# A graph layer on one TensorE: rounds of edges set around the halves of layer 1 and layer 2, with a reordered front and a last block of one part

## The reference, cut to what matters

```python
agg = segment_sum(edge_attr, receivers, num_segments=6250)      # 106250 edges x 128, receivers sorted
h   = relu(layernorm(x))                                        # 6250 nodes x 128
out = x + relu(concatenate([agg, h], axis=1) @ W1 + b1) @ W2 + b2   # W1 256x512, W2 512x128
```

## Time and profile before

| | before |
|---|---|
| median of 3 runs | 207.87 us (207.56 to 207.99) |
| the profiled execution, its own time | 207.57 us |
| its span, first to last instruction | 205.8 us |
| PE busy | 193.6 us, 94% |
| DVE busy | 131.8 us, 64% |
| ACT busy | 85.6 us, 42% |
| POOL busy | 44.5 us, 22% |
| DMA moved | 62.49 MB, mean 304 GB/s |
| granted TensorE clock, mean | 0.993 of full |

### The profile page before, as it was taken

One profiled execution on the slowest core, in us unless ns is written; L12 is line 12 of the kernel. 1 busy time (PEld: TensorE's weight loads), 2 busy tenths in 40 slices (PEclk: granted clock), 3 DMA queues, 4 the chain that ended last, 5 costly groups with the idle time before them and its releaser, 6 DMA issues.

```text
span 205.8 us, 6846 instructions
## 1 busy us (share of the span) xinstructions
PE 193.6 (94%) x2580; PEld 166.7 (81%) x2580; DVE 131.8 (64%) x582; ACT 85.6 (42%) x187; POOL 44.5 (22%) x121
## 2 busy tenths in 40 slices
PE   5979699999999999999999999999998999999990
PEld 5668588887898898898887987988987988978990
DVE  2665948776778669577677777786782884853200
ACT  3324434643714713823634544337137137126030
POOL 6973022102210220222022022012202012200000
PEclk9999999999999999999999999999999999999997
DMA  6999999999999999999999999999998970010100
GB/s 210 380 375 376 361 374 377 377 374 384 385 377 385 377 372 392 377 379 389 376 392 377 381 386 377 371 347 372 348 376 311 299 250 12 3 52 0 51 24 21
DMA packets 44497, 62.49 MB, mean 304 GB/s; under 512 B 1796, under 2 KB 44168, under 8 KB 44462
## 3 DMA queue, kind: packets, MB, share of 16 engines
q1 hardware_dynamic: 44132, 61.66, 84.5%
q10 hardware_dynamic: 330, 0.36, 0.7%
HBM read 58.81 MB, written 3.20 MB: 301 GB/s over the span
## 4 chain that ended last, share of the span: by engine, by line
PE 82%; DMA 7%; POOL 3%; DVE 2%; ACT 2%; issue 1%; DVEq 0%; POOLq 0%
PE bank L916 22%; PE bank L850 20%; PE bank L887 17%; PE bank L897 16%; DMA edges<-in_edge_attr 6%; PE bank L861 4%; PE bank L871 2%; DMA hidden<-in_dst 2%; POOL aggT L390 1%; POOL rstd L370 1%; PE bank L843 1%; ACT hidden L448 1%; DVE aggT L617 1%; POOL var L365 1%; ACT xn L417 0%
## 5 line engine op out<-in xcount | busy, mean ns | idle before, releaser
L850 PE MATMUL bank<-edges,onehot 128*32 128x128 f32 x1656 | 52.5, 277 | 1.4 <-DMA edges<-in_edge_attr 0.9
L850 PEld LDWEIGHTS bank<-edges,onehot 128*32 128x32 f32 x1656 | 43.6, 110 | 8.2 <-issue 5.0
L617 DVE TENSOR_TENSOR aggT<-bank,aggT 128x32 f32 x277 | 35.7, 190 | 22.3 <-issue 10.3
L448 ACT ACTIVATE hidden<-bank,b_col 128x512 f32<-128x512 f32 (+2 forms) x56 | 34.2, 633 | 36.8 <-PE bank L897 36.7
L916 PE MATMUL bank<-w,hidden 128*128 128x128 f32 (+1 forms) x400 | 48.4, 278 | 0.0
L916 PEld LDWEIGHTS bank<-w,hidden 128*128 128x128 f32 (+1 forms) x400 | 45.8, 189 | 2.5 <-issue 2.2
L417 ACT ACTIVATE xn<-xs,shift,rstd 128x128 f32<-128x128 f32 (+1 forms) x50 | 21.8, 484 | 49.2 <-POOL shift L372 49.2
L365 POOL TENSOR_SCALAR var<-meanvar 128x2 f32<-128x2 f32 (+1 forms) x25 | 8.4, 334 | 128.2 <-DVE meanvar L544 128.1
L524 DVE TENSOR_TENSOR onehot<-relT,iota 128x384 f32<-128x384 f32 x69 | 34.5, 550 | 0.0
L897 PE MATMUL bank<-agg_hi,w_hi 128*128 128x512 f32 (+2 forms) x56 | 21.6, 385 | 1.6 <-DVE agg_lo L566 1.6
L887 PE MATMUL bank<-hT_hi,w_hi 128*128 128x512 f32 (+2 forms) x56 | 22.1, 394 | 0.2 <-DVE hT_lo L560 0.2
(11 more groups left out here) (101 smaller groups left out, 181.3 us busy)
## 6 DMA issues: line engine op xcount, KB each, us to landing
edges<-in_edge_attr SPq DMA_DIRECT2D x69, 768.0 KB, 10.6
xs<-in_x SPq DMA_DIRECT2D x21, 128.0 KB, 9.7
out_rows<-w SPq DMA_DIRECT2D x5, 256.0 KB, 10.1
out_rows<-outrow SPq DMA_DIRECT2D x5, 256.0 KB, 9.9
w<-in_L_gnn_W SPq DMA_DIRECT2D x3, 256.0 KB, 10.6
out_rows<-outrow SPq DMA_DIRECT2D x3, 128.0 KB, 8.4
xs<-in_x SPq DMA_DIRECT2D x1, 256.0 KB, 5.8
hidden<-in_dst SPq DMA_DIRECT2D x1, 192.0 KB, 3.1
```

What stands on the lines that cost most here:

```text
L448: nc.scalar.activation(hidden[:, t, 0:cols], hidden_of(s, t), ACT.Relu, bias=b1_col[:, t:t + 1]).then_inc(hidden_ready, 1)
L617: nc.vector.tensor_tensor(win, turn_ps[:, at:at + W], win, ALU.add).then_inc(agg_added, 1)
L850: ins = nc.tensor.matmul(sums_ps[t * W:(t + 1) * W, cols], onehot[:, hots, e, :], edges[:, slot, e * F:(e + 1) * F], start=(g == 0), stop= ...
```

## The change

Three things. In steps 5 to 24 one round comes first, then half of layer 2 or of `layer1_h`, then the other rounds, then the second half. The front (steps 0 to 4, with ACT's, DVE's and POOL's order there) is reordered: six idle transposes go, layer 2 of groups 1 and 2 is cut in two parts around a step's end, and POOL clears less before the second block's statistics. The last block gets one node to a partition: one part of 106 rows, and its store is 96 rows and 10 rows. The wait for `over_read` moves behind the first round of step 20.

```diff
-    assert NLAST % 2 == 0 and NB % 2 == 1
+    assert NLAST <= P and NB % 2 == 1
+    LAST_CUT = NLAST // 16 * 16
     def width(b):
-        return NLAST // 2 if isinstance(b, int) and b == NB - 1 else P
+        return NLAST if isinstance(b, int) and b == NB - 1 else P
+    def parts(b):
+        return 1 if isinstance(b, int) and b == NB - 1 else 2
...
-                    sp.dma_start(out_last_v, rows[0:width(NB - 1), 1, :]).then_inc(done, 16)
+                    sp.dma_start(out_last_v[0:LAST_CUT, :], rows[0:LAST_CUT, 1, 0:F]).then_inc(done, 16)
+                    sp.dma_start(out_last_v[LAST_CUT:NLAST, :], rows[LAST_CUT:NLAST, 1, 0:F]).then_inc(done, 16)
...
             clear(0, 2)
             spread(0)
-            clear(2, 6)
+            clear(2, 3)
             spread(1)
-            clear(6, CLEARS)
+            clear(3, CLEARS)
...
             h_out(1)
+            copy_sums(0)
+            round_w1(0)
             act.wait_ge(b2_spread, 1)
...
-            copy_sums(0)
-            round_w1(0)
...
+                if k == 1:
+                    h_out(2)
                 if group1(k) is not None:
                     relu(group1(k), group1(k))
-                if k == 1:
-                    h_out(2)
...
             build(1)
+            turned_ab(0, rel_copied, 4 * TILES, P)
             stats(1)
...
-            turned_ab(0, rel_copied, 4 * TILES, P)
             relative(2, dstC, colC, relC)
             relative(3, dstD, colD, relD)
-            rest_of_h(1)
             dve.wait_ge(rel_turned, 2)
             turned_ab(1, rel_copied)
+            rest_of_h(1)
...
-            def layer2(n, s):
-                if not (isinstance(n, int) and n == 0):
+            def layer2(n, s, first=0, last=2, only=None):
+                if not (isinstance(n, int) and n == 0) and first == 0 and only != 1:
                     pe.wait_ge(out_added, n)
...
-                at = 0
+                at = first * P
                 for i, b in enumerate(blocks_of(s)):
                     w = width(b)
+                    if only == 1 - i:
+                        at += nodes(b)
+                        continue
...
-                    for j in range(2):
+                    for j in range(first, min(last, parts(b))):
...
-            sum_rounds(0, 2, 3)
+            sum_rounds(0, 2, 4)
...
-            sum_rounds(0, 3, 4)
-            pe.wait_ge(rel_copied, 2)
-            layer1_h(1, 1, 0, 2)
             pe.wait_ge(rel_copied, 3)
             turn_sums(0)
+            layer1_h(1, 1, 0, 2)
...
-                if k == FLAG + 1:
-                    pe.wait_ge(over_read, 1)
                 if k == 1:
                     sum_rounds(1, 0, 1)
-                    idle(6, tr_ps)
+                    turn_x(2)
                     pe.wait_ge(w1_ready, 2)
                     layer1_agg(0, 0, 1)
-                    sum_rounds(1, 1, 2)
-                    turn_x(2)
-                    sum_rounds(1, 2, 4)
-                    layer1_h(2, 2)
+                    sum_rounds(1, 1, 4)
+                    layer1_h(2, 2, 0, 2)
                     turn_sums(1)
+                    layer1_h(2, 2, 2, 4)
                 elif k <= EARLY:
-                    layer2(two, two)
+                    if k == 2:
+                        layer2(two, two)
+                    else:
+                        layer2(two, two, 1, 2)
                     sum_rounds(k, 0, 2)
                     layer1_agg(one, one, blocks_of(one)[-1] + 1)
                     sum_rounds(k, 2, 4)
                     turn_x(k + 1)
+                    layer2(one, one, 0, 1)
                     turn_sums(k)
+                elif k == EARLY + 1:
+                    layer2(two, two, 1, 2)
+                    sum_rounds(k)
+                    turn_sums(k)
+                    turn_x(k + 1)
                 else:
-                    sum_rounds(k)
+                    sum_rounds(k, 0, 1)
+                    if k == FLAG + 1:
+                        pe.wait_ge(over_read, 1)
                     if two is not None:
-                        layer2(two, two)
+                        layer2(two, two, only=0)
                     if one is not None:
-                        layer1_h(one, one)
+                        layer1_h(one, one, 0, 2)
+                    sum_rounds(k, 1, 4)
+                    if two is not None:
+                        layer2(two, two, only=1)
+                    if one is not None:
+                        layer1_h(one, one, 2, 4)
                     turn_sums(k)
```

More of the change, by code:

```diff
@@ L96, in cols_of @@
     def cols_of(s):
-        return sum(2 * width(b) for b in blocks_of(s))
+        return sum(nodes(b) for b in blocks_of(s))
     def alone(s):
@@ L104, in place @@
         first = BLOCK if b >= ONES and (b - ONES) % 2 else 0
-        return slice(first, first + 2 * width(b))
+        return slice(first, first + nodes(b))
     with ExitStack() as ctx:
@@ L163, in graph_layer @@
         limit_i = early[:, 4 * CHUNK:4 * CHUNK + 3]
-        b2_row = sums[0:1, 0, 0:F]
-        ones = sums[0:1, 1, 0:P]
+        b2_row = hidden[0:1, 3, P:2 * P]
+        ones = hidden[0:1, 3, 2 * P:3 * P]
         outrow_2 = w1[:, 1, :].rearrange("p (a n) -> p a n", a=2)
@@ L415, in normalise @@
                     act.wait_ge(h_turned, b - 1)
-                for j in range(2):
+                for j in range(parts(b)):
                     ins = nc.scalar.activation(xn[0:w, par, j, :], xs[0:w, b, j * F:(j + 1) * F], ACT.Relu,
@@ L437, in round_agg @@
                     act.wait_ge(hidden_summed, n * HT)
-                nc.scalar.activation(agg_hi[:, halves].rearrange("f (j p) -> f j p", j=2),
+                j = parts(b)
+                nc.scalar.activation(agg_hi[:, halves].rearrange("f (j p) -> f j p", j=j),
                                      aggT[:, bass.ds(b * BLOCK, halves.stop - halves.start)
-                                          ].rearrange("f (p j) -> f j p", j=2), ACT.Copy).then_inc(agg_hi_ready, 1)
+                                          ].rearrange("f (p j) -> f j p", j=j), ACT.Copy).then_inc(agg_hi_ready, 1)
             def relu(n, s):
@@ L495, in again_group @@
                     for i, b in enumerate(blocks_of(s)):
-                        round_agg(b, FULL + 1, slice(i * BLOCK, i * BLOCK + 2 * width(b)), n)
+                        round_agg(b, FULL + 1, slice(i * BLOCK, i * BLOCK + nodes(b)), n)
                     relu(n, s)
@@ L541, in stats @@
                     dve.wait_ge(rstd_ready, b - 1)
-                dve.wait_ge(halves_ready, 2 * b + 2)
-                for j in range(2):
+                dve.wait_ge(halves_ready, 2 * b + parts(b))
+                for j in range(parts(b)):
                     ins = nc.vector.bn_aggr(meanvar[0:w, par, j, :], halves[0:w, par, j, :])
@@ L551, in add_b2 @@
                     dve.wait_ge(b2_ready, 1)
-                r = xs[0:w, b, :].rearrange("p (j f) -> p j f", j=2)
-                nc.vector.tensor_tensor(r, r, b2_all[0:w, :].unsqueeze(1).to_broadcast([w, 2, F]),
+                j = parts(b)
+                r = xs[0:w, b, 0:j * F].rearrange("p (j f) -> p j f", j=j)
+                nc.vector.tensor_tensor(r, r, b2_all[0:w, :].unsqueeze(1).to_broadcast([w, j, F]),
                                         ALU.add).then_inc(residual_ready, 1)
             def rest_of_h(b):
-                w = width(b)
+                n = nodes(b)
                 dve.wait_ge(hT_hi_ready, b + 1)
-                cols = slice(b * BLOCK, b * BLOCK + 2 * w)
-                nc.vector.tensor_tensor(hT_lo[:, cols], tr_ps[:, 0:2 * w], hT_hi[:, cols].bitcast(F32),
+                cols = slice(b * BLOCK, b * BLOCK + n)
+                nc.vector.tensor_tensor(hT_lo[:, cols], tr_ps[:, 0:n], hT_hi[:, cols].bitcast(F32),
                                         ALU.subtract).then_inc(hT_lo_ready, 1)
@@ L588, in finish @@
                     dve.wait_ge(last_summed, 1 if n < NS else 2)
-                    nc.vector.tensor_tensor(rows[0:w, 1, :], last_ps[0:w, 0:2 * F], xs[0:w, bs[1], :],
+                    nc.vector.tensor_tensor(rows[0:w, 1, 0:F], last_ps[0:w, 0:F], xs[0:w, bs[1], 0:F],
                                             ALU.add).then_inc(last_added, 1)
@@ L691, in _ @@
                 rest_of_agg(k - 1, k - 1, place(k - 1))
+                if k == 1:
+                    rest_of_h(2)
                 if 2 <= k <= EARLY:
@@ L802, in again_group @@
                     for i, b in enumerate(blocks_of(s)):
-                        rest_of_agg(NB + b, b, slice(i * BLOCK, i * BLOCK + 2 * width(b)))
+                        rest_of_agg(NB + b, b, slice(i * BLOCK, i * BLOCK + nodes(b)))
                     finish(n, s)
@@ L920, in layer2 @@
                         ins.then_inc(out_summed, 1)
-                ins.then_inc(last_summed if ends else out_summed, 1)
+                if last == 2 and only != 0:
+                    ins.then_inc(last_summed if ends else out_summed, 1)
```

33 lines of the change are left out of this document (18 added, 15 removed).

## The result

The changed kernel takes 210.53 us, the median of 4 runs (210.36 to 211.11), against 207.93 us for the kernel before in the same comparison: the ratio is 1.0113, with a 95% interval from 1.0077 to 1.0150 (the quotient of the two medians, 1.0125, lies in it). The forecast was 209.8 us, in a range of 207.2 to 212.6. Slower was right. PE's part of it came within 0.3 us of the sum; the end gave back less than forecast.

A forecast was written before the change was run, and what follows sets the result against it. PE's serial work was taken to bound the middle of the kernel. Terms of +6.0 + 0.3 - 0.75 - 0.5 - 0.9 - 0.1 - 2.1 = +1.95 us led to 209.8 us, range 207.2 to 212.6.

The forecast's parts named there:

- The bound: From 48 to 153 us PE is always busy, so a microsecond added to its work there adds one to the total.
- The interleaving: Steps 6 to 23: changes between rounds and layers cost PE 0.33 us in each of 18 steps, +6.0 us.
- The term for a second start: In each interleaved step, starting a layer's second half holds PE 0.11 us longer.
- The wait that is moved closer: Rounds end later, so `copy_sums` and `round_agg` behind it leave DVE's chain to `agg_lo` no slack: +0.3 us.
- The rival of a bound DVE: Late `copy_sums` makes each of nine pairs wait for `agg_lo`: 4.5 us instead of 0.3, 214 us; chance 0.13.
- The front: Steps 0 to 5: fewer idle transposes and waits, `layer1_agg` of step 5 at 51.1: -0.75 us.
- The overrun test: Step 20: a round of 0.80 us now stands ahead of PE's 0.53 us wait and covers it: -0.5 us.
- The last block and the end: Eight fewer PE instructions in layer 2, -0.9; a reshaped last addition, -0.1; 96 stored rows side by side, -2.1 us.
- The bound of -0.5 for rows in line: Last store: if 96 rows went over two engines only, 48 in a line take 2.6 us, gaining only 0.5 us.
- The range: Whole kernel: 207.2 to 212.6 us given, from term bounds of 207.6 and about 213.
- That the changes are hidden: Rival: added changes of work cost PE under 0.225 us a step, in full 203.5 us, faster; chance 0.12.
- That the front gives nothing: Rival: steps 0 to 5 gain nothing, or lose it to the DMA engines: 210.5 us; chance 0.15.

The follow-up runs named there:

- e1: Changed kernel with steps 5 to 24 in the old form, all rounds and then whole layers: 205.05 us, ratio 0.9858.
- e2: Kernel before with only the rounds set around the halves in steps 5 to 24: 213.37 us, ratio 1.0266.
- e12: Changed kernel with whole layers again, plus an unread 128-column transpose behind the first round of steps 6 to 23: 212.83 us, ratio 1.0257.
- e6: Changed kernel with all rounds of a step first, then the two halves of the layer right behind each other: 204.89 us.
- e5: Changed kernel with ACT's `round_agg(k - 1)` ahead of `copy_sums(k)` in steps 5 to 24: 210.70 us.
- e11: Changed kernel with ACT's `round_agg(k - 1)` ahead of `copy_sums(k)` from step 6 on, not in step 5: 210.42 us, ratio 1.0139.
- e4: Kernel before with only the reordered steps 0 to 4: 208.06 us, ratio 1.0028.
- e3: Kernel before with only the last block as one part of 106 rows, stored as 96 and 10 rows: 205.27 us, ratio 0.9879.
- e10: Changed kernel with halves in step 5 alone and the last 10 rows issued by ACT beside SP's 96: 204.24 us, ratio 0.9850.
- e9: Changed kernel with halves in step 5 alone and the last 106 rows in one store: 203.93 us, ratio 0.9811.

## Why the prediction was right, point by point

**The bound.** PE's time was the kernel's time. Shown: e1 and e2 take and give what the count of changes says, on both bases, and e12 adds 7.8 us with 18 transposes of 0.11 us each. Shown with it is that the price hangs on going from rounds to other work and back. What in that change costs it (the narrower weights, the four strips of output, or another difference between the two kinds of product) no run separates.

**The interleaving, +6.0.** Right. The four runs of a step came out within 0.02 us of the sum's terms. The term for a second start, 0.11, was put beside the changes of work as if it were a thing of its own; e6 shows that it is not paid without rounds between the halves. The number was right, since in this kernel it only occurs together with them.

**The wait that is moved closer, +0.3.** Right in kind and place: `layer1_agg` starts late in steps 7, 9 and 13, by 0.18, 0.11 and 0.21 us over the usual gap, 0.5 in all. e5 and e11 show the cause, the order of ACT's queue, and not a lack of DVE time. The rival of a bound DVE falls with them. The prediction had about four pairs without slack; three of the nine wait.

**The front, -0.75.** It was -0.67, at 51.18 where 51.1 was forecast. And DVE's side sets it, as forecast: in the changed kernel the chain to this point runs from the landing of a store at 48.58 over `finish` and the sums to `agg_lo` at 50.70, and PE waits for that. The term had the front and step 5's own halves in one. e2 and e4 part them: e4 shows that the reordered steps 0 to 4 give nothing while whole layers stand in step 5, and e2 that halves in step 5 give 0.56 of the 0.67 with the old front; the halves there are what turns the wait for edges into work. This one place is where the interleaving pays.

**The overrun test, -0.5.** The wait at step 20 is gone: the first round starts at 161.87, 0.10 us after the last small transpose before it, where it was 0.70. That is 0.6 us.

**The last block and the end, -0.9, -0.1 and -2.1.** The first two hold (the eight instructions are 1.0 us, and the 0.3 us of step 23 was not in the sum). The third is the term that was mis-sized: measured at -0.8 in the changed kernel and -1.0 in e3. Two of its parts failed. The second issue was taken 0.3 us behind the first, as the issue of 53 or 128 rows takes 0.28 to 0.35; the issue of the 96 rows took 0.74 us here and between 0.71 and 2.36 in the others, so the second came 0.78 later. And 1.4 us from issue to landing was read from the end of the data in the earlier trace rows, not from the end of a wait; from the second issue to the end of the wait it is 0.39 + 1.9 = 2.3 us. e10 shows that this second part is no matter of a second issue on SP. The bound of -0.5 for rows in line was too dear as well: it took the time of 1 KB packets for rows that are now 512 B, and the 53 in a line of e9 move in 1.4 us, where the sum had 2.6 for 48. The "2 for 106 rows" of "DMA: Bandwidth & Descriptors" in the Trainium skill fits e9's 1.4 us of 512 B packets in two lines.

What stays open is why the issue of 96 rows takes so long, and why SP's wait ends later behind the last row in e6 than in e9. The issue follows a 128-row store by 0.4 us in every case, as the single store of 106 rows does, which takes 0.29. The shape and the number of rows differ, and no run here tells these from other causes.

**The range.** Its upper end is given as about 213, but the terms given for it (6.5 and 1.5, less 0.5, 0.9, 0.1 and 2.1) make 4.4 us over 207.87, which is 212.3. For the interleaving the two ends use 5.0 and 6.5, not its own bounds of 2.5 and 7.2.

**Rivals.** That the changes are hidden: refuted by e1, e2 and e12. That DVE's chain becomes the bound: refuted, 0.5 us of it exists. That the front gives nothing: true of the front by itself (e4), not with step 5's halves.

## What to carry to other kernels

When an engine is full, price every change between two kinds of work on it, not only the work: runs of one, two and three of the same piece in the old trace gave 0.14 us to a hundredth. Spread work out only at the place where something is waited for; here it was one step of twenty. At the end of a kernel, read the time from the issue to the end of the wait, not to the last packet: in the traces, one store whose rows moved in line (2.4 us) beat a cut one whose rows moved side by side (2.8 to 3.7 us).

## What the runs showed of the hardware that was not expected

Going from products with 32-column weights to one product with 128-column weights and back costs 0.29 us at full clock (e12), two and a half times as long as the product itself. The issue of a store of 96 rows of 512 B behind one of 128 rows of 1 KB took 0.71 to 2.36 us on SP in different executions, that of 106 rows of 512 B took 0.29 us. The last rows of both moved 2.1 us after the first issue in e6 and e9, and SP's wait ended 0.7 us later with two stores and 0.3 us later with one.
